# Weights of set-up products laid out transposed by the host in a decoder-layer kernel

## What is computed

```python
x = _layernorm(x + _L0_attn_ref(x, ...))                       # A: convolution, sin/cos moments, running sums
x = _layernorm(x + _L0_xattn_ref(x, ctx_1024, ctx_1024, ...))  # B: autocorrelation through Fourier transforms
x = _layernorm(x + _L0_ffn_ref(x, ...))                        # C: gated experts, below
...
Q = x @ W_Q.T
K = x @ W_K.T
invQ = Q @ W_inv.T
invK = K @ W_inv.T
fwd = _fused_branch(Q, K, V_fwd, W_fwd, U_fwd, b_fwd, router_w1, router_b1, router_w2, ...)
inv = _fused_branch(invQ, invK, W_inv_exp, V_inv, U_inv, b_inv, router_w1, router_b1, router_w2, ...)
out = fwd + alpha_bi * inv
return out @ W_O.T
```

## Time and profile before

| | us |
|---|---|
| median of 3 runs | 960.15 |
| lowest and highest | 957.73, 961.58 |
| the profiled execution | 960.6 |
| its span in the trace | 958.7 |
| TensorE busy in the span | 865.2 |
| VectorE busy | 766.4 |
| ScalarE busy | 537.6 |
| GpSimd busy | 96.2 |

### The profile page before, as it was taken

How to read it: one execution, slowest core, us unless ns; L and a number is a source line. 1 busy time by engine, 2 the same in 40 slices (tenths; PEclk the granted TensorE clock), 3 DMA queues, 4 the chain that set the end, 5 groups by cost and what they waited for, 6 DMA issues and landing times.

```text
span 958.7 us, 11672 instructions
## 1 busy us (share of the span) xinstructions
PE 865.2 (90%) x4056; PEld 510.3 (53%) x4056; DVE 766.4 (80%) x1290; ACT 537.6 (56%) x875; POOL 96.2 (10%) x174
## 2 busy tenths in 40 slices
PE   3569865999999999999999999999999999997896
PEld 1134633663665556564756466555655475656345
DVE  5796888989878999899979997899879995373231
ACT  3484892677448673767467755856475655311310
POOL 2010011300120011100210011100200021001000
PEclk9679996999999999999999999999999999999898
DMA  9742034110432024100611044001510150000000
GB/s 292 133 89 44 6 83 88 46 45 0 83 72 67 0 48 85 66 23 13 120 45 45 1 91 107 23 0 35 120 44 1 23 111 23 1 1 23 0 1 22
DMA packets 41214, 50.81 MB, mean 53 GB/s; under 512 B 14843, under 2 KB 34374, under 8 KB 41158
## 3 DMA queue, kind: packets, MB, share of 16 engines
q0 software_dynamic: 7008, 25.21, 13.9%
q1 hardware_dynamic: 34006, 24.48, 8.9%
q10 hardware_dynamic: 144, 0.39, 0.1%
HBM read 20.68 MB, written 4.19 MB: 26 GB/s over the span
## 4 chain that ended last, share of the span: by engine, by line
PE 71%; DVE 18%; ACT 6%; issue 3%; POOL 1%; DMA 1%; ACTq 0%; DVEq 0%; SPq 0%; POOLq 0%
PE ps L797 12%; PE ps L778 10%; PE ps L769 9%; PE ps L653 6%; PE ps L593 5%; PE ps L735 5%; PE ps L576 4%; DVE sc L2569 3%; PE ps L623 3%; PE ps L712 3%; PE ps L637 3%; DVE zc L2490 2%; PE ps L436 2%; DVE sc L2561 2%; PE ps L702 2%
## 5 line engine op out<-in xcount | busy, mean ns | idle before, releaser
L2569 DVE TENSOR_TENSOR_SCAN sc<-mask,sc 128x1024 f32<-128x1024 bf16 x64 | 146.2, 2284 | 0.4
L778 PE MATMUL ps<-x2t,mv 128*128 128x512 f32 x256 | 123.7, 606 | 0.3 <-DVE prod L2818 0.3
L769 PE MATMUL ps<-cum,mw 128*128 128x512 f32 x256 | 122.1, 599 | 0.3 <-ACT cs L1646 0.2
L797 PE MATMUL ps<-up,prod 128*128 128x256 f32 x512 | 115.6, 381 | 1.3 <-DVE prod L2818 1.2
L797 PEld LDWEIGHTS ps<-up,prod 128*128 128x128 f32 x512 | 94.7, 190 | 18.9 <-issue 4.8
L2325 POOL DMA_DIRECT2D acc<-sq x48 | 42.1, 877 | 567.9 <-ACT sq L1552 567.9
L1646 ACT ACTIVATE cs<-ps 128x512 f32<-128x512 f32 x64 | 38.0, 594 | 99.8 <-PE ps L769 95.0
L2561 DVE TENSOR_TENSOR sc<-sc,g 128x1024 f32<-128x1024 f32 x64 | 77.3, 1208 | 7.4 <-ACT sc L1536 7.3
L2490 DVE SCALAR_TENSOR_TENSOR zc<-ps,cst,zc 128x510 f32<-128x510 f32 (+2 forms) x96 | 71.3, 742 | 13.7 <-ACT zc L1463 11.4
L769 PEld LDWEIGHTS ps<-cum,mw 128*128 128x128 f32 x256 | 47.4, 191 | 63.6 <-issue 59.5
L593 PE MATMUL ps<-sc,wy 64*64 64x512 f32 x512 | 66.1, 638 | 10.9 <-DVE sc L2569 10.9
(11 more groups left out here) (263 smaller groups left out, 1478.1 us busy)
## 6 DMA issues: line engine op xcount, KB each, us to landing
acc<-sq POOLq DMA_DIRECT2D x48, 512.0 KB, 4.6
xa<-in_x_dram SPq DMA_DIRECT2D x8, 512.0 KB, 4.4
xs_a<-in_x_dram SPq DMA_DIRECT2D x8, 512.0 KB, 3.6
cin<-in_ctx_dram SPq DMA_DIRECT2D x8, 512.0 KB, 4.6
out_dram<-prod SPq DMA_DIRECT2D x8, 512.0 KB, 3.0
win<-in_in_proj_dram SPq DMA_DIRECT2D x1, 544.0 KB, 6.6
prod<-in_L_ffn_V_fwd_dram SPq DMA_DIRECT2D x2, 256.0 KB
prod<-in_L_ffn_W_fwd_dram SPq DMA_DIRECT2D x2, 256.0 KB
```

Of the source, the lines that this page charges most:

```text
L769: last = mm(o, mw[:, t, br, c:c + P], cum[:, t, :], start=(t == 0), stop=(t == 1))
L778: last = mm(o, mv[:, t, br, c:c + P], x2t[:, t, :], start=(t == 0), stop=(t == 1))
L797: mm(d, prod[:, j, q * P:(q + 1) * P], up[:, j, :], start=(j == 0), stop=False)
L2569: V.tensor_tensor_scan(flat, mask[:, 0:2 * T], flat, 0.0, ALU.mult, ALU.add)\
```

## The change

The host transposes W_O, W_inv and router_w1, pads the transposed router_w2 to 32 columns, and stacks, transposes and tiles the two bias tables to 128 columns. The kernel loads these five into the places where the transposed results stood. The eight transposing folds go, on TensorE and on ScalarE, so FOLD has 26 entries; two zeroing writes on GpSimd go, and the counts of the semaphore `zeroed` go down by two. The rest of the diff is order: all five queues are rearranged, from chunk 0 to chunk 7.

```diff
-        for dst, src in ((fq, f_q), (fk, f_k), (fo, f_o), (fi, f_inv), (fr, r_w1)):
+        for dst, src in ((fq, f_q), (fk, f_k), (fot, f_ot), (fit, f_invt), (frt, r_w1t),
+                         (w2t[:, :, :], r_w2t), (bt, b_both)):
             LOADS_RAW += [(dst, src.rearrange("(t p) n -> p t n", p=P))]
...
-        LOADS_RAW += [(rw2, r_w2), (b16[0:KEXP, :], b_fwd), (b16[KEXP:2 * KEXP, :], b_inv),
-                      (selraw, select), (rb1[:, :], r_b1.rearrange("(t p) -> p t", p=P)),
+        LOADS_RAW += [(selraw, select), (rb1[:, :], r_b1.rearrange("(t p) -> p t", p=P)),
...
-            sp.wait_ge(zeroed, 7)
+            sp.wait_ge(zeroed, 5)
...
-        FOLD = ([("bo", 0)] + [(m, t) for m in ("ot", "it", "rt") for t in range(DT)] + [("w2", 0), ("bt", 0)]
-                + [(m, t) for m in ("nq", "nk") for t in range(DT)]
+        FOLD = ([("bo", 0)] + [(m, t) for m in ("nq", "nk") for t in range(DT)]
                 + [(m, br, t) for m in ("mv", "mw", "mr") for br in range(2) for t in range(DT)]
                 + [("up", j) for j in range(NJ)] + [("bp", 0)])
...
-            for t in (rb2[:, :], w2t[:, :, :], bt, bp[:, :], wcols[:, :, :], bsel[:, :, :], brow[:, :, :]):
+            for t in (rb2[:, :], bp[:, :], wcols[:, :, :], bsel[:, :, :], brow[:, :, :]):
...
+    for name in ("L0_ffn_W_O", "L0_ffn_W_inv", "L0_ffn_router_w1"):
+        given[name] = np.ascontiguousarray(given[name].T)
+    w2 = np.pad(given.pop("L0_ffn_router_w2").T, ((0, 0), (0, 32 - KEXP)))
+    b_both = np.tile(np.concatenate([given.pop("L0_ffn_b_fwd"), given.pop("L0_ffn_b_inv")]).T, (1, P // (2 * KEXP)))
```

More of the change, by code:

```diff
@@ L933, in _ @@
             c_own(0, 4)
+            b_wt(1)
             c_running(0, 5)
@@ L936, in _ @@
             c_own(0, 5)
+            b_wf(1)
             c_running(0, 6)
             c_spread(0, 6)
-            b_wt(1)
-            b_wf(1)
             c_own(0, 6)
+            a_sums(2, 1)
             c_running(0, 7)
-            a_sums(2, 1)
             c_spread(0, 7)
@@ L1009, in _ @@
             c_own(1, 6)
-            b_wt(2)
             c_running(1, 7)
             c_spread(1, 7)
+            b_wt(2)
             c_own(1, 7)
+            a_sums(3, 1)
             b_wf(2)
@@ L1069, in _ @@
             c_spread(2, 4)
+            a_sums(4, 0)
             c_own(2, 4)
@@ L1133, in _ @@
             c_spread(3, 2)
+            a_sums(5, 0)
             c_own(3, 2)
@@ L1136, in _ @@
             c_spread(3, 3)
+            b_wt(4)
             c_own(3, 3)
             c_running(3, 4)
+            b_wf(4)
             c_spread(3, 4)
-            b_wt(4)
             c_own(3, 4)
@@ L1143, in _ @@
             c_spread(3, 5)
-            b_wf(4)
             c_own(3, 5)
             c_running(3, 6)
+            b_back(4)
             c_spread(3, 6)
-            a_sums(5, 1)
             c_own(3, 6)
@@ L1152, in _ @@
             c_own(3, 7)
-            b_back(4)
+            a_sums(5, 1)
             c_out(3, 0)
             c_out(3, 1)
-            b_out(4, 0)
-            b_out(4, 1)
             a_sums(5, 2)
             a_sums(5, 3)
+            b_out(4, 0)
             a_squares(5)
-            b_transform(5, "cf", 0)
-            b_transform(5, "cf", 1)
+            b_out(4, 1)
             a_factor(5, 0)
             a_factor(5, 1)
-            c_transpose(4, 0)
-            c_transpose(4, 1)
             a_transpose(6, 0)
@@ L1170, in _ @@
             a_scores(6)
+            a_project(6, 0)
             a_out(5, 1)
+            b_transform(5, "cf", 0)
+            b_transform(5, "cf", 1)
+            c_transpose(4, 0)
+            c_transpose(4, 1)
+            a_project(6, 1)
             c_hidden(4, 0)
-            a_project(6, 0)
-            a_project(6, 1)
             c_hidden(4, 1)
@@ L1262, in _ @@
             c_weights(5)
-            a_project(7, 3)
+            a_sums(7, 0)
             c_spread(5, 0)
@@ L1271, in _ @@
             c_own(5, 2)
-            a_sums(7, 0)
             c_running(5, 3)
-            b_wt(6)
             c_spread(5, 3)
@@ L1282, in _ @@
             c_spread(5, 5)
+            b_wt(6)
             c_own(5, 5)
             c_running(5, 6)
+            b_wf(6)
             c_spread(5, 6)
-            b_back(6)
             c_own(5, 6)
@@ L1291, in _ @@
             a_sums(7, 1)
+            b_back(6)
             c_out(5, 0)
@@ L1345, in _ @@
             c_running(6, 7)
+            b_wt(7)
             c_spread(6, 7)
@@ L1697, in _ @@
             a_turns(0, 6)
+            fold(1)
             a_squares(0, 2)
@@ L1701, in _ @@
             a_squares(0, 3)
-            fold(1)
+            a_angles(0, 6)
             fold(2)
@@ L1795, in _ @@
             a_transpose(2, 1)
+            b_layer(0)
             a_scores(2)
-            b_layer(0)
+            c_transpose(0, 0)
+            c_transpose(0, 1)
+            a_layer(1)
             a_exp(2)
             a_project(2, 0)
-            c_transpose(0, 0)
-            c_transpose(0, 1)
             c_hidden(0, 0)
+            c_hidden(0, 1)
+            b_transform(1, "cf", 0)
             a_project(2, 1)
-            a_layer(1)
-            c_hidden(0, 1)
             c_hidden(0, 2)
+            a_turns(2, 0)
             c_hidden(0, 3)
-            a_turns(2, 0)
             a_turns(2, 1)
@@ L3132, in _ @@
             a_moments(4, 6)
+            b_back(3)
             a_scan(4, 6)
@@ L3179, in _ @@
             c_scale(3, 2)
+            b_weight(4)
             c_prod(3, 2)
```

867 lines of the change are left out of this document (405 added, 462 removed).

## The result

The changed kernel took **954.05 us** (median of 9 runs, 952.57 to 956.69) against 960.25 us in the 9 runs of the kernel before that were made with it (955.82 to 961.58). The ratio is **0.9945, 95% interval 0.9925 to 0.9965**: faster by 0.55%, between 0.35 and 0.75%. The forecast was 956.1. The profiled execution took 953.27 us, its span is 951.4, 7.3 us less than before.

What follows compares the result with a forecast made beforehand. Chunk 0's engine-to-engine chain bounds 60 to 180 us, TensorE 180 to 800, then the last chunk's stage C. 960.6 less 1.7 (start) less 2.8 (gap at 240 us) gives 956.1 us; range 950 to 962.

Steps and rivals of the forecast that it cites:

- Removed steps, 2.3 us: Chunk 0's start: fourteen of sixteen removed transposes stood on TensorE's chain from 59.16 to 61.43, so 2.3 us go.
- Moved products, a_squares(0) from 82.18 to 80.5: Chunk 0's start: three products fill TensorE's idle stretch (2.9 us saved), two others move before a_squares (2.8 us added).
- the floor of 80.4 at VectorE: Chunk 0's start: a_squares(0) cannot end before VectorE's last a_both at 79.39 plus 0.99 us.
- From a_squares on each step waits for one before it ... I keep 1.7: From a_squares(0) to the full stage: the 1.7 us won at the start last to the end.
- bias_parts "0, upper end 1": GpSimd: bias_parts, moved ahead of a_accumulate(1,5), barely fits into the wait there; cost 0, at most 1 us.
- The gap at 240 us, -2.8: TensorE before b_wf(1): the new order closes the gap, 1.2 us of idle and 1.6 of half clock.
- The rule against the row: Gap at 240 us: by the skill's rule it gives 1.2 us, by the profile's half clock 2.8; forecast took 2.8.
- The boundaries open too: Rival: the gap at 690.92 goes and that at 796.34 shrinks to 1.5, 6.0 us more, 950.1 us; chance 0.20.
- The slower rival: ScalarE between chunks: b_layer(0) and a_layer(1) ahead of a_exp(2) delay a_spread(2,0), TensorE stops; 969.1 us, chance 0.10.
- The last stage: After 880 us: chunk 7's last stage should take its 78.7 us unchanged.
- The signs: Trace marks: a_squares(0) ends at 80.5, bp copy at 111.7, c_hidden(0,0) about 183, no wait near 238, idle about 13.5.

Runs made afterwards that it cites:

- e1: Kernel before with only the eight transposing steps and their copies removed, all else in place: 959.92 us, ratio 0.9998.
- e2: Kernel before with the new layout and the changed kernel's TensorE, ScalarE and VectorE order up to the last folded product: 957.26 us, ratio 0.9974.
- e10: Changed kernel with VectorE's biases() cut in three and products 12 and 13 behind a_squares(0) and a_factor(0,0) on TensorE: 950.39 us, ratio 0.9911 to before.
- e3: Kernel before, transposing steps and start order kept, with the changed kernel's order behind the last folded product on all queues: 954.96 us, ratio 0.9956.
- e5: Changed kernel with two products moved into TensorE's gap between a_squares(0) and a_factor(0,0): 950.77 us, ratio 0.9916 to the kernel before.
- e7: Changed kernel with bias_parts on GpSimd back behind rstd(0,1): 957.16 us, ratio 0.9980 to the kernel before.
- e6: Kernel before, transposes kept but moved with three products into the idle stretch ahead of a_sums(0,1), other products as in the changed kernel: 957.01 us, single execution.
- e8: e5 with bias_parts back behind rstd(0,1) and b_wt(0) ahead of a_squares(1,6) on ScalarE: 955.37 us, ratio 0.9953 to the kernel before.
- e9: e5 with bias_parts behind rstd(1,0) on GpSimd and the copy of wtt ahead of a_squares(1,6): 953.16 us, ratio 0.9929 to the kernel before.
- e11: e10 with the two later edits of e9: 951.94 us, ratio 0.9923 to the kernel before.
- e4: Kernel before with one TensorE line moved, b_wf(1) behind c_own(0,6) instead of right behind b_wt(1): 958.19 us, ratio 0.9983.

## Why the prediction was right or wrong

The total came out as forecast within 2 us (956.1 against 954.05), though by other terms, and that their sum fits is partly luck: the forecast took 1.7 us from the start and 2.8 from one gap, the ratios give 1.1 to the start and 4.2 to the later order.

- **Removed steps, 2.3 us: wrong.** The step said "fourteen ran on the chain". They did, in the sense that nothing else filled these 2.3 us; but the next a_sums waits for VectorE's scan until 63.0 whether they run or not. e1 measured 0. The trace of before had it: the products ahead of that a_sums ended at 63.42 (61.43 and 1.99), and the scan at 63.28. As the a_sums of e1 starts 0.15 us behind its scan, nothing was to be had. VectorE before the change:

```profile
61.00 2.28 DVE L2569 TENSOR_TENSOR_SCAN sc<-mask,sc 128x1024 f32<-128x1024 bf16 x1
```

- **Moved products, a_squares(0) from 82.18 to 80.5: right, by the wrong split.** It ended at 80.2, and the floor of 80.4 at VectorE was real. All of it is the order's, as e2 shows beside e1. The floor itself was put down to VectorE, and e10 shows the accumulating DMA close under it.
- **"From a_squares on each step waits for one before it ... I keep 1.7": this step failed.** Two products, 2.8 us, had filled the wait between a_squares(0) and a_factor(0,0). The forecast moved them away as a cost of the stretch in front and did not ask what they had covered: TensorE stood idle for 2.35 us and went to half clock. Against the kernels with the old start (e1 and e3: a_squares(0) ends at 81.8, a_scores(1) starts at 89.6) the changed kernel is 1.5 us early at a_squares(0) and 0.8 at a_scores(1), and e2 1.6 early and then level. b_heads(0) beside bias_parts gave back 0.9 more. The mechanism, a gain that lasts once it is past the ramp, was right: e5 and e10 carry theirs whole from 182 to 785 us. In the ratios the start brought 2.5 us with the old later order (e2) and 1.1 with the new one (0.9956 against 0.9945, intervals that overlap), in the traces 0.7 and 0.3. So the runs do not refute the size of 1.7, the single traces speak for less, and the reason given for it is refuted.
- **bias_parts "0, upper end 1": mis-sized, and with the wrong sign.** It did fit ahead of a_accumulate(1,5), and it cost VectorE 0.9 us by contention, as the upper end had it. But its move was needed: left in its place, the new order of ScalarE stops TensorE (e7, some 3 us slower). It was costed against the old order's neighbours alone.
- **The gap at 240 us, -2.8: right that it closes, mis-sized.** The idle 1.2 us went. The 1.6 us of half clock behind it (1.7 by the marks) came in that execution and not in others: e1, e2 and e6 keep the gap of 1.24 us and have no fall there. With one fall in four the term is 1.2 + 0.4 = 1.6 us, an estimate.
- **The rule against the row.** The Trainium skill (TensorE: Matmul & The Clock Gate, "Why this matters for your kernels") warns of gaps above about 3 us. The forecast read from it that shorter ones cost themselves alone, and took the other side because of one fall behind one gap. The runs side with neither: gaps of 0.8 to 2.4 us had a fall behind them in part of the executions and none in the others. Behind the gap near 105 us, where it was above 3 us (3.7, in e5, e8 and e9), the clock fell each time, which agrees with the warning.
- **"The boundaries open too", given 0.20: nearest to what happened after 280 us.** The gap of 1.85 us at 691 went and that of 2.37 at 796 shrank to 1.00, as that rival had it, and the clock fell more rarely. e3 measured 4.2 us for the later order where the forecast had 2.8 and the rival 8.8.
- **The slower rival, given 0.10:** its place was right, ScalarE between chunks 1 and 2, with a_layer(1) ahead of exp. a_spread(2,0) was not late in the changed kernel. e7 is that rival at work, with 3.16 us of stop and a fall of the clock, once rstd(1,0) is late.
- The last stage took 72.6 us from c_transpose(7) (72.7 before): unchanged, as forecast.
- **The signs.** Three products at 43.97, the bp copy at 111.9 (111.7 forecast), no wait at 238 and 11.67 us idle (13.5 or less) came true. Two did not: c_hidden(0,0) started at 184.74 instead of about 183, as the start's 1.7 us had not lasted, and an idle stretch of over 1 us with half clock behind it opened at 82.6 us, where none had been.

Not settled: why the clock falls in one execution and not in another with the same order and gaps, and whether filling the gap at 82 us makes the fall rarer or only the wait shorter. Nor why it fell behind the wait near 105 us in eight of the nine profiled executions without the transposing steps (not in e11, which has a fall at 112) and in none of the four with them (before, e3, e4, e6), though that wait is 1.9 to 3.7 us long in the nine and 1.9 to 2.3 in the four. No run separates this from the rest of the start.

## What to carry to other kernels

A step between two that wait is worth nothing until you have found what the second of them waits for once the step is gone; removed in place, eight of them gave 0 here, and what paid was the freedom to put others into idle time. When work is moved forward, look at the hole that it leaves, not only at the queue that it joins: 2.35 us opened behind a_squares(0), and refilling it gave some 3 us by the ratios, of which part may be chance, where the removal alone gave none. And a helper's work on a side engine (bias_parts) must be costed with the new order of everything that waits behind it.

## What the runs showed of the hardware

- TensorE's granted clock falls from its upper level (2.4 GHz, 1.00) to 1.2 GHz (0.50) behind gaps of 0.8 to 2.4 us, but not every time: at the same 1.24 us near 240 us in 1 of 4 profiled executions (before, not e1, e2, e6), at the 1.85 us near 690 in 3 of 5 (before, e2, e4, not e1, e6), at the 2.37 us near 794 in 4 of 5 (not e2), at 1.18 us in the last stage in 5 of 11. Two profiled executions can so differ by some 5 us of 960 in the full stage that neither the work nor the idle time explains, and by 2 to 3 us in the last.
- Small operations of VectorE and GpSimd side by side slow each other: 128x32 operations took 0.43 to 0.72 us instead of 0.23 to 0.25 beside GpSimd's 128x256 copies, and a 128x4 multiplication of GpSimd 2.27 instead of 0.20 us beside a scan of VectorE.
- An accumulating DMA of 512 KB took 4.8 us from issue to landing at the start (median of the two in e10), so the squares' sums land later than VectorE could take them: with its small operations out of the way it waited 1.95 us for them.
